# Layer-norm forms moved between VectorE, ScalarE and GpSimd in a fused scan, router and expert kernel

## The reference, cut to what matters

```python
x = x + mamba(_layernorm(x))      # L0_attn_a
x = x + ffn(_layernorm(x))        # router and 16 experts, top 6
x = x + attention(_layernorm(x))  # L0_attn_b
x = x + ffn(_layernorm(x))        # the same router and experts

# mamba(x)
xn = layernorm(x, in_norm_alpha, in_norm_bias)
x_in, z = split(xn @ in_proj_w.T + in_proj_b)
x_conv = silu(causal_conv4(x_in) + conv_b)
Bm, Cm = split(x_conv @ x_proj_w.T + x_proj_b)
delta = clip(softplus(x_conv @ dt_proj_w.T + dt_proj_b), 1e-4, 10)
# per token: h = exp(clip(delta*A,-10,0))*h + delta*Bm*x_conv; every 16th token
# h is scaled back to norm 10; y = Cm.h + D*x_conv        (512 channels x 16 states)
out = (y * silu(z)) @ out_proj_w.T + out_proj_b
return layernorm(residual + out, norm_alpha, norm_bias)

# layernorm(x, alpha, bias): alpha*(x-mean)/(std+1e-6) + bias, std with n-1
# ffn: softmax of router logits, top 6 probabilities normalised to gates,
# out = sum over experts of gate[e] * (x @ expert_w[e])
```

## Time and profile before

| | us |
|---|---|
| median of 3 runs | 4976.51 (4974.76 to 4981.58) |
| the profiled execution | 4979.03, its span 4977.2 |
| pipeline loop, 314 to 3022 | 2708: PE busy 2461, DVE 2382, POOL 2271, ACT 2117 |
| last 64 tiles, 3610 to 4977 | 1367: PE busy 1238, DVE 827, ACT 290 |
| mean of the granted TensorE clock | 0.952 |

### The profile page before, as it was taken

The page is one execution under the profiler, slowest core; times in us unless marked ns, Lnnn a source line. Parts: engine busy times, 40 slices in busy tenths (PEclk is TensorE's granted clock), DMA queues, the critical chain, the costliest instruction groups (busy, mean ns, idle before and its releaser), DMA issues.

```text
span 4977.2 us, 83341 instructions
## 1 busy us (share of the span) xinstructions
PE 4396.3 (88%) x22592; PEld 3061.0 (62%) x22592; DVE 3774.0 (76%) x9556; ACT 2928.0 (59%) x8578; POOL 2691.3 (54%) x1412
## 2 busy tenths in 40 slices
PE   5899998899989998999899989877776779999999
PEld 4777777777777776777677777634434444444444
DVE  3898988888888888888889889953333357777776
ACT  5877787777777777778777778724444421111111
POOL 3888888888888888888888888810000000000000
PEclk8999999999999999999999999988888989999999
DMA  2111111111111111111111111100100100000000
GB/s 95 53 54 49 52 50 52 48 50 51 52 51 47 55 48 55 45 53 49 53 49 53 50 53 49 50 31 26 51 25 30 42 25 19 17 19 18 17 19 16
DMA packets 119406, 214.06 MB, mean 43 GB/s; under 512 B 19232, under 2 KB 85664, under 8 KB 118560
## 3 DMA queue, kind: packets, MB, share of 16 engines
q1 hardware_dynamic: 119072, 211.10, 12.9%
HBM read 184.83 MB, written 26.21 MB: 42 GB/s over the span
## 4 chain that ended last, share of the span: by engine, by line
PE 39%; issue 19%; DVE 17%; POOL 16%; ACT 6%; DMA 1%; DVEq 1%; SPq 1%; POOLq 0%; ACTq 0%
PE ps L644 21%; POOL prod L342 8%; POOL hb L350 5%; DVE macc L957 3%; ACT zr L408 3%; PE ps L771 3%; PE ps L695 2%; PE ps L621 2%; PE ps L674 2%; PE ps L750 2%; DVE sc L1108 1%; DVE dtt L1113 1%; PE ps_dA L771 1%; PE ps L681 1%; POOL u L359 1%
## 5 line engine op out<-in xcount | busy, mean ns | idle before, releaser
L644 PE MATMUL ps<-w_x,mxT 128*128 128x512 f32 x4096 | 1893.1, 601 | 21.8 <-DVE macc L957 21.8
L864 DVE TENSOR_TENSOR_SCAN hb<-ps_dA,hb 128x1088 f32<-128x1088 f32 x512 | 1240.6, 2423 | 164.7 <-issue 103.3
L342 POOL TENSOR_TENSOR prod<-hb,cbc 128x1024 f32<-128x1024 f32 x512 | 1120.2, 2188 | 408.4 <-DVE hb L883 408.4
L408 ACT ACTIVATE zr<-dt,aneg 128x128 f32<-128x128 f32 x4096 | 1240.8, 388 | 69.8 <-DVE dt L1007 69.8
L350 POOL TENSOR_TENSOR hb<-u,bbc 128x1024 f32<-128x1024 f32 x512 | 1199.7, 2343 | 84.2 <-POOL prod L342 72.1
L644 PEld LDWEIGHTS ps<-w_x,mxT 128*128 128x128 f32 x4096 | 745.7, 193 | 725.3 <-issue 654.2
L957 DVE SCALAR_TENSOR_TENSOR macc<-ps,gate,macc 128x256 f32<-128x256 f32 x2048 | 977.5, 477 | 246.9 <-PE ps L644 180.5
L621 PEld LDWEIGHTS ps<-prod,ident 128*128 128x128 f32 x8192 | 979.1, 198 | 254.0 <-POOL prod L342 194.2
L621 PE MATMUL ps<-prod,ident 128*128 128x128 f32 x8192 | 997.1, 282 | 142.5 <-POOL prod L342 142.5
L417 ACT ACTIVATE ps_dA<-zr 128x1024 f32<-128x1024 f32 x512 | 518.3, 1012 | 0.0
L424 ACT ACTIVATE sq<-hb 128x64 f32<-128x64 f32 x512 | 159.6, 312 | 450.8 <-DVE hb L864 447.2
(11 more groups left out here) (184 smaller groups left out, 5014.3 us busy)
## 6 DMA issues: line engine op xcount, KB each, us to landing
bbc<-bcd SPq DMA_DIRECT2D x128, 512.0 KB, 3.8
cbc<-bcd SPq DMA_DIRECT2D x128, 512.0 KB, 3.5
xt<-in_x SPq DMA_DIRECT2D x128, 128.0 KB, 3.0
x2d<-macc SPq DMA_DIRECT2D x64, 128.0 KB, 1.7
xcv<-x2d SPq DMA_DIRECT2D x64, 128.0 KB, 2.1
x3d<-x1b SPq DMA_DIRECT2D x64, 128.0 KB, 1.9
x1b<-x3d SPq DMA_DIRECT2D x64, 128.0 KB, 2.0
out_dram<-macc SPq DMA_DIRECT2D x64, 128.0 KB, 1.7
```

The source lines that it names most:

```text
L342: TT(dst, states, cc, ALU.mult).then_inc(M["prodp"], 1)
L408: last = act(zr[k][:, s, :], dt[:, s // N, :], ACT.Relu, bias=10.0, scale=aneg[:, s:s + 1])
L644: last = mm(banks[p % len(banks)][:], mxT[k][:, j, :], w_x[:, j, p * 512:(p + 1) * 512], start=(j == 0), stop=(j == KD - 1))
L864: V.tensor_tensor_scan(states, dA, states, 0.0, ALU.mult, ALU.add).then_inc(M["scan"], 1)
```

## The change

- Set-up: two TENSOR_TENSORs with broadcast operands build the diagonal matrices in place of 20 TENSOR_SCALARs.
- xn and mxn are formed by ScalarE, as Identity with scale 1/std and bias -mean/std, at the head of chunk 0. VectorE forms that bias for xn (nx, chunk 7) and -mean for mxn (nmm, behind `route_norm1`); ScalarE multiplies it (nmr).
- VectorE: o1 stands in chunk 0 behind dt; selp stands with the gate in chunk 7; `route_norm1` stands in chunk 7 behind dtt; L1108 is a TENSOR_SCALAR with a pointer scalar. The router's steps are counted anew.
- The closing norm: o3 is (x - mean) * alpha and o4, new, in chunk 4 behind xcc, is x / std + bias, both SCALAR_TENSOR_TENSOR on VectorE. GpSimd's two forms go, and its x1 stands in chunk 7.
- ScalarE: L501 and L503 stand at the head of chunk 3; in chunk 7 the softplus stands ahead of `route_norm`; ScalarE writes out two more steps and so enters its loop one turn on (`first=6`, 27 turns).

```diff
-        def pipeline(eng, step):
-
-
-            for i, stages in ((-3, "L"), (-2, "LF"), (-1, "LFG"), (0, "LFGS"), (1, "LFGSB"), (2, "LFGSBX"), (3, "LFGSBXY")):
-                step(i, i % 2, stages)
-            with eng.Fori(2, NTILES // 2 - 2) as j:
+        def pipeline(eng, step, first=4):
+
+            edge = {-3: "L", -2: "LF", -1: "LFG", 0: "LFGS", 1: "LFGSB", 2: "LFGSBX", NTILES - 3: "FGSBXY",
+                    NTILES - 2: "GSBXY", NTILES - 1: "SBXY", NTILES: "BXY", NTILES + 1: "XY", NTILES + 2: "Y"}
+            for i in range(-3, first):
+                step(i, i % 2, edge.get(i, "LFGSBXY"))
+            with eng.Fori(first // 2, NTILES // 2 - 2) as j:
...
-            for i, stages in ((NTILES - 4, "LFGSBXY"), (NTILES - 3, "FGSBXY"), (NTILES - 2, "GSBXY"), (NTILES - 1, "SBXY"),
-                              (NTILES, "BXY"), (NTILES + 1, "XY"), (NTILES + 2, "Y")):
-                step(i, i % 2, stages)
+            for i in range(NTILES - 4, NTILES + 3):
+                step(i, i % 2, edge.get(i, "LFGSBXY"))
...
-                if c == 4 and "B" in stages:
-                    g.wait_ge(M["o3"], AHEAD + i)
-                    TT(oo[:], oo[:], ga_row[:], ALU.mult).then_inc(M["o4"], 1)
+                if c == 7 and "B" in stages:
...
-                    TT(oo[:], oo[:], be_row[:], ALU.add).then_inc(M["o5"], 1)
-                if c == 6 and "B" in stages:
-                    g.wait_ge(M["o5"], AHEAD + i)
...
+                a.wait_ge(R["nmm"], AHEAD + n + 1)
+                a.wait_ge(R["rs"], AHEAD + n + 1)
+                act(ms[:, 14:15], ms[:, 13:14], ACT.Identity, scale=ms[:, 1:2]).then_inc(R["nmr"], 1)
+
+            def route_norm2(n, k):
+                a.wait_ge(R["nmr"], AHEAD + n + 1)
+                a.wait_ge(R["xT"], AHEAD + n)
+                act(mxn[:], mxt[k][:], ACT.Identity, bias=ms[:, 14:15], scale=ms[:, 1:2]).then_inc(R["xn"], 1)
...
                 for c in range(NC):
+                    if c == 0 and F:
+                        a.wait_ge(M["nx"], AHEAD + i + 3)
+                        a.wait_ge(M["xnT"], AHEAD + i + 2)
+                        act(xn[:], xt[0][:], ACT.Identity, bias=sc[:, 13:14], scale=sc[:, 7:8]).then_inc(M["xn"], 1)
+                    if c == 0 and X_:
+                        route_norm2(i - 2, k)
+                    if c == 3 and B:
+                        a.wait_ge(M["vc3"], AHEAD + i)
+                        act(sc[:, 9:10], sc[:, 8:9], ACT.Ln).then_inc(M["ln3"], 1)
+                        a.wait_ge(M["ln3"], AHEAD + i)
+                        act(sc[:, 10:11], sc[:, 9:10], ACT.Exp, scale=0.5).then_inc(M["sd3"], 1)
                     if S_:
...
-                        if B:
-                            a.wait_ge(M["vc3"], AHEAD + i)
-                            act(sc[:, 9:10], sc[:, 8:9], ACT.Ln).then_inc(M["ln3"], 1)
-                            a.wait_ge(M["ln3"], AHEAD + i)
-                            act(sc[:, 10:11], sc[:, 9:10], ACT.Exp, scale=0.5).then_inc(M["sd3"], 1)
...
                     if c == 7:
-                        if B:
-                            route_norm(i - 1)
                         if F:
...
                             act(dtt[:], dtt[:], ACT.Ln, bias=1.0).then_inc(M["ldt"], 1)
+                        if B:
+                            route_norm(i - 1)
                         if X_:
...
-            pipeline(a, step)
+            pipeline(a, step, first=6)
...
+                    route_norm2(n, k)
...
-            pe.wait_ge(s_zero, EB * (TAPS + 1) + 1)
+            pe.wait_ge(s_zero, 3)
...
-
-            def route_norm2(n, k):
-                v.wait_ge(R["rs"], AHEAD + n + 1)
-                v.wait_ge(R["xT"], AHEAD + n)
-                TS(mxn[:], mxt[k][:], mmv[:, 0:1], ms[:, 1:2], ALU.subtract, ALU.mult).then_inc(R["xn"], 1)
+                v.wait_ge(R["mv"], AHEAD + n + 1)
+                v.wait_ge(R["nmr"], AHEAD + n)
+                TS(ms[:, 13:14], mmv[:, 0:1], -1.0, None, ALU.mult).then_inc(R["nmm"], 1)
...
-                if F:
-                    v.wait_ge(M["sx1"], AHEAD + i + 3)
-                    v.wait_ge(M["xnT"], AHEAD + i + 2)
-                    TS(xn[:], xt[0][:], mv[:, 0, 0:1], sc[:, 7:8], ALU.subtract, ALU.mult).then_inc(M["xn"], 1)
-                if X_:
-                    route_norm2(i - 2, k)
...
+                if B:
+                    v.wait_ge(M["xr"], AHEAD + i * 16)
+                    v.wait_ge(M["x1"], AHEAD + i - 1)
+                    STT(oo[:], xt[1][:], r1b[1 - k][:], ob_row[:], ALU.mult, ALU.add).then_inc(M["o1"], 1)
...
-                if B:
-                    v.wait_ge(M["xr"], AHEAD + i * 16)
-                    v.wait_ge(M["x1"], AHEAD + i - 1)
-                    STT(oo[:], xt[1][:], r1b[1 - k][:], ob_row[:], ALU.mult, ALU.add).then_inc(M["o1"], 1)
...
-                    TS(oo[:], oo[:], mv[:, 2, 0:1], sc[:, 12:13], ALU.subtract, ALU.mult).then_inc(M["o3"], 1)
+                    STT(oo[:], oo[:], mv[:, 2, 0:1], ga_row[:], ALU.subtract, ALU.mult).then_inc(M["o3"], 1)
...
+                if B:
+                    v.wait_ge(M["o3"], AHEAD + i)
+                    STT(oo[:], oo[:], sc[:, 12:13], be_row[:], ALU.mult, ALU.add).then_inc(M["o4"], 1)
...
                     V.bn_stats(st[:, 0, :], xt[0][:]).then_inc(M["st1"], 1)
+                end(5)
+
+                start(6)
                 router(5, 6)
-                end(5)
-
-                start(6)
-                router(6, 7)
                 if L_:
...
                     V.bn_aggr(mv[:, 0, :], st[:, 0, :]).then_inc(M["mv1"], 1)
-                router(7, 8)
+                router(6, 7)
                 if L_:
...
                 halfway(6)
-                router(8, 10)
+                router(7, 9)
                 end(6)
...
                 start(7)
-                if B:
-                    route_norm1(i - 1, 1 - k, lambda: v.wait_ge(M["x1"], AHEAD + i))
-                router(10, 11)
+                router(9, 10)
                 halfway(7)
...
                     v.wait_ge(M["qs"], AHEAD + i + 4)
-                    STT(sc[:, 6:7], sc[:, 4:5], 1e-6, sc[:, 5:6], ALU.mult, ALU.add).then_inc(M["den"], 1)
+                    TS(sc[:, 6:7], sc[:, 4:5], 1e-6, sc[:, 5:6], ALU.mult, ALU.add).then_inc(M["den"], 1)
                 if F:
...
                             .then_inc(M["dtb"], 1)
+                if B:
+                    route_norm1(i - 1, 1 - k, lambda: v.wait_ge(M["x1"], AHEAD + i))
                 if L_:
                     v.wait_ge(M["den"], AHEAD + i + 4)
+                    v.wait_ge(M["xn"], AHEAD + i + 3)
                     V.reciprocal(sc[:, 7:8], sc[:, 6:7]).then_inc(M["sx1"], 1)
-                router(11, 12)
+                    v.wait_ge(M["sx1"], AHEAD + i + 4)
+                    TS(sc[:, 13:14], mv[:, 0, 0:1], sc[:, 7:8], -1.0, ALU.mult, ALU.mult).then_inc(M["nx"], 1)
+                router(10, 11)
                 if X_:
...
-            for e in range(EB):
-                for t in range(TAPS):
-                    TS(dcw[:, e * TAPS + t, :], ident[:], cw[:, e, t:t + 1], None, ALU.mult).then_inc(s_zero, 1)
-                TS(ddp[:, e, :], ident[:], dpar[:, e:e + 1], None, ALU.mult).then_inc(s_zero, 1)
+            for dst, w in ((dcw, cw[:].rearrange("p e t -> p (e t)")), (ddp, dpar[:])):
+                n = dst.shape[1]
+                TT(dst[:], ident[:].rearrange("p (a c) -> p a c", a=1).broadcast_to([P, n, P]),
+                   w.rearrange("p (a c) -> p a c", c=1).broadcast_to([P, n, P]), ALU.mult).then_inc(s_zero, 1)
             V.memset(hb[0][:, :, 0:1], 0.0)
...
             V.memset(carry[:, NT // 2 - 1:], 0.0).then_inc(s_zero, 1)
-            v.wait_ge(s_zero, EB * (TAPS + 1) + 1)
+            v.wait_ge(s_zero, 3)
             pipeline(v, step)
...
-                        if more and e == 1:
-                            route_norm2(i + n0 + 1, 1 - k)
...
-                            top(i + 1, 1 - k, range(2 * (e - 9), min(2 * (e - 8), 13)))
+                            top(i + 1, 1 - k, range(2 * (e - 9), min(2 * (e - 8), 12)))
...
-                route_norm2(n0, 0)
...
-                top(0, 0, range(13))
+                top(0, 0, range(12))
```

## The result

The changed kernel takes 4808.19 us (median of 4 runs, 4803.30 to 4811.38) against 4976.10 (4 runs): ratio 0.966, interval 0.9643 to 0.9676. First the page of after: span, part 1, and one line of part 3 (queue: packets, MB, share of the span).

The account below looks back on a forecast made before the run. No engine was full; GpSimd holding VectorE forms, TensorE's chain and GpSimd from S5 to S7 ended the waits. Odd tile 1.14 plus even 0.57, 31 pairs x 1.71 = 53 us, set-up and fill 0: 4925 us, range 4868 to 4975.

Parts of the forecast that it names:

- S1 to S5: Second to sixth scan start of a tile: TensorE's chain pins it, and o4 behind L1066 adds 0.34 us in both tiles.
- S0 to S1: First to second scan start of a tile: xn and mxn leave VectorE, saving 0.20 us (odd) and 0.33 (even).
- S5 to S7: Sixth to eighth scan start: selp leaves, GpSimd alone needs 10.9 us; saves 1.09 us (odd) and 0.48 (even).
- S7 to the next S0: Eighth scan start to the next tile's first: reduction waits for ScalarE's squares; saves 0.19 us (odd) and 0.10 (even).
- den: One-element VectorE form L1108 in chunk 7, behind the reduction: 0.13 us where it was 1.03.
- ScalarE's cover: At the tile's edge: ScalarE's added nmr, xn and mxn stay hidden before its next squares, with about 1.1 us to spare.
- the loop one turn later: 0: ScalarE's loop, entered one turn later with 26 branches back in place of 27: costs 0, bounds -1 and +5.
- the set-up's line: Before the loop: 20 forms of 4.0 us become 2560 elements at 2.9, saving 1.1 us.
- Rival 1: Even tile's convolution: shorter pauses around the branch keep TensorE's clock, worth about 56 us, time 4869; chance 0.13.
- Rival 2: Chunk 7 grows by dependent small forms and o4 meets GpSimd: 0.3 + 0.25 us a tile back, 4959; chance 0.20.
- Rivals 3 and 4: 3: TensorE bounds the tile and takes the gain, 4976, chance 0.06. 4: ScalarE becomes the bound, 5009, chance 0.08.

Follow-up runs that it names:

- e11: The changed kernel plus ten unread one-column memsets in VectorE's set-up, so its loop starts at instruction 590 as before the change: 4923.8 us.
- e14: The changed kernel with o1 put back in chunk 1, run on the same chip as the unedited changed kernel: 4790.6 us.
- e9: The changed kernel with den (chunk 7) again a scalar_tensor_tensor with two tensor operands, same number of VectorE instructions: 4878.7 us.
- e2: The kernel before, with only ScalarE writing out two more steps and entering its loop one turn on: 4973.0 us.
- e6: The kernel before with nine fewer VectorE set-up instructions (taps of three channel blocks in one form each), loop starting at 581: 4864.8 us.
- e10: The kernel before with VectorE's short set-up of 2 forms and eight unread one-column memsets behind it, loop starting at 580: 4865.0 us.
- e1: The kernel before with only VectorE's set-up shortened to 2 forms in place of 20, loop starting at 572: 5025.9 us.

## Why the prediction was wrong, step by step

e11 has the change's forms and the loop at its old place, and took 4923.8 us; the forecast was 4925. So the forecast went wrong by what it held fixed, which was the branch and the clock behind it. That e11 meets it to 1 us is partly luck: the even tile's 0.50 better in S1 to S5 and 0.20 worse in S7 to S0 offset other errors. The table has stretches in us (S0–S1 and so on, means):

| | odd: before, e11 | saved, forecast | even: before, e11 | saved, forecast |
|---|---|---|---|---|
| S0–S1 | 5.99, 5.86 | 0.13, 0.20 | 4.98, 4.73 | 0.25, 0.33 |
| S1–S5 | 22.86, 23.25 | -0.39, -0.34 | 24.91, 24.75 | 0.16, -0.34 |
| S5–S7 | 11.98, 10.90 | 1.08, 1.09 | 11.41, 10.90 | 0.51, 0.48 |
| S7–S0 | 11.12, 10.99 | 0.13, 0.19 | 7.06, 7.16 | -0.10, 0.10 |
| tile | 51.95, 51.00 | 0.95, 1.14 | 48.36, 47.54 | 0.82, 0.57 |

A turn saves 1.77, forecast 1.71. Step by step:

- **S0 to S1** held: dt takes the stretch and o1 0.47. That o1 costs about 0.33 a tile here and that its leaving chunk 1 gives nothing back was in the sum, and e14 measures it: 21 us over 64 tiles.
- **S1 to S5** held in the odd tile: L1067 still waits for TensorE's chain, and o4 stands behind it. In the even tile S1 to S4 fell from 17.84 to 17.27, and S4 to S5, behind the matmuls at half clock, rose from 7.07 to 7.48: a gain of 0.16 where a loss of 0.34 was forecast.
- **S5 to S7** held to 0.03: 10.90 in both tiles.
- **S7 to the next S0** held within 0.2, but not by its terms. The reduction started at S7 + 3.64 in the odd tile, forecast 3.65. The ten steps behind it that the prediction lists add up to 2.84 and not to the 2.97 that it carries on; with 2.84 its forecast would have been 8 us lower, 4917. Neither size was right: from the reduction to the next scan, without the branch, e11 takes 3.77 and 3.35 (odd, even) where before took 3.29 and 2.84, so 0.5 longer where 0.18 was forecast. In the odd tile e11's shorter branch (3.58, before 3.82) hides half of that. den, forecast at 0.90 a tile (1.03 less 0.13), measures about 1.1 (e9).
- **ScalarE's cover** held, and so did "the loop one turn later: 0": in the kernel after it waited 1.41 us (odd) and 0.91 (even) for the scan at the tile's edge, forecast 1.1, and e2 is the kernel before to 0.01%.
- **The step that failed** stands in the paragraph on what bounds the kernel and in the set-up's line. The 103.3 us in the earlier trace rows and the 3.72 in the earlier trace rows were named as the branches' and then carried through unchanged, and the set-up was priced by its work alone (1.1 us, which is what the work measures: the forms took 4.00 us before and 2.88 after). Nothing in the prediction asked why a branch takes 3.7 us. Its term was missing: VectorE's loop moves from 590 to 580, and with that 3.53 us a turn go at the branch (10.99 to 7.46) and 1.51 at the clock (S4 to S5 of the even tile, 7.48 to 5.97), while the even tile's chunk 0 gets 0.98 longer (4.73 to 5.71). That the others no longer catch up in a pause ahead of it is the likely reason, not shown by a run. With 0.15 elsewhere that is 4.21 a turn, 27 turns 114 us; after and e11 differ by 115.6. By itself, on the kernel before, it is 108 and 110 (e6, e10). 168 us are then 108 for the place and, from e6 to after, 57 for the forms, with 3 of scatter.
- **Rival 1**, the kept clock, came true in its effect and not by its cause. The moved forms did shorten the even tile's pause before L674 (2.89 before, 2.35 in e11, in the mean), but that did not keep the clock: in e11 L685 is slow in 24 of 27 even tiles (before, 26), and L1068 waited 79.7 us for the convolution. With the branch's pause gone as well it is 0.89 in the kernel after, and slow in none. Its price of 56 us is what S4 to S5 gives (7.07 to 4.99 in e6, 27 times); the even tile as a whole got only 0.63 shorter by it, 17 us.
- **Rival 2**, chunk 7 grows, came in part: the late squares and the slower chain both held, which is the 0.3 a tile above, but o4 ran in 0.47 in the tile shown and cost no more. Rivals 3 and 4 did not come: TensorE didn't take the gain, and ScalarE had room.

What stays open: why the refetch costs between 2.8 and 5.2 us by place, what lies ahead of the program so that the cuts fall at 576 and not at 512 or 640, and why with o1 in chunk 0 the wait for GpSimd two scans on is 0.3 longer.

## What to carry to other kernels

A wait on "issue" once per turn of a loop was a fetch here (and in e1 the profile put it down to another engine): look at the packets of the instruction queue, count each engine's loop in the built program, and shift it with a few small instructions ahead of it until the packets in the loop are gone; here that was worth 108 to 116 us of 4976, twice the tuning of the forms (51 to 57). Any edit of straight code ahead of a loop moves the loop, so its price is not that of its own work, and a comparison between two kernels can carry this step of 2 to 3% unless the packets are looked at. Beside a busy GpSimd, the tiny VectorE form took 0.2 us with one tensor operand and with two lasted until GpSimd's form ended. Moving such a form pays by where it stands: 65 us for selp, and minus 21 for o1, which left a stretch that TensorE bounds.

## What the runs showed of the hardware

- VectorE and ScalarE fetch instructions in packets of 8192 bytes. VectorE's loops inside three pieces of 128 instructions cost 0.21 us at the branch; those over four cost 2.8 to 5.2 us. On ScalarE, which had room, a loop over four pieces cost nothing to be seen.
- Eight memsets that nothing reads made a kernel 161 us faster (5025.9 to 4865.0).
- A late branch on VectorE can cost twice: TensorE's pause behind it (3.16 us in the earlier trace rows, 1.41 in the tile shown of after) was followed by matmuls at half speed, and the granted clock of the even tiles was 0.938 in the mean, in place of 0.987. A low clock by itself is no loss: in e6 an even tile has 1.98 us at half clock in chunk 0, and S4 to S5 is still 4.99.
- A one-element form with two tensor operands beside GpSimd took 1.28 us, and 0.20 with one; with two it ended 0.02 us after GpSimd's form did, in 63 of 64 tiles.
